# Another order in the slots of the last transformer: rotary sums on GpSimd, roots on ScalarE, the down product one slot later

## The chip, the core and the metric

The kernel runs on one core of one Trainium2 chip. The metric is the device time of one execution in microseconds (us), and runs are compared by their median. TensorE (PE in the profile; PEld are its weight loads), VectorE (DVE), ScalarE (ACT), GpSimd (POOL) and SyncE (SP, which issues DMAs) each carry out their own list of instructions in order. They wait for one another with semaphores, on which an instruction counts up when it has ended.

## The reference

Four layers follow one another on x of 4 x 512 tokens and 128 features. Each computes `x = x + attention(xn) * silu(ffn(xn))`, where xn is the layer norm of x. The change touches only the "ffn" of layer 3, counted from 0, which is itself a transformer of two layers with 8 heads of 64, windows of 64 tokens and a gated feed-forward product. Cut to what matters:

```python
def _layer(x, wqkv, qs, ksc, wo, lg, lb, w1, b1, w2, b2):
    h = shift_token(x)                    # half of the features come from the token before
    q, k, v = jnp.split(h @ wqkv, 3, axis=-1)
    q, k, v = (to_heads(q), to_heads(k), to_heads(v))
    q = l2norm(q) * qs                    # t / max(norm(t), 1e-12)
    k = l2norm(k) * ksc
    q, k = rotary_xpos(q, k)              # q * cos * scale + rotate_half(q) * sin * scale; k with 1 / scale
    o = local_attention(q, k, v)          # softmax over the own window and the one before
    x = x + o @ wo
    h = shift_token(x)
    h = (h - mu) / jnp.sqrt(var + 1e-05) * lg + lb
    a, g = jnp.split(h @ w1 + b1, 2, axis=-1)
    x = x + (a * gelu(g)) @ w2 + b2
    return x
```

## The kernel before

All data are float32. `transformer` is called once, by `ffn3`, with depth 2, 8 heads, window 64 and a hidden width of 341 (three chunks, `HC`). The 2048 tokens are 16 tiles of 128. With 8 heads a tile is one group (`NG == 1`), so the two layers make 32 groups, numbered n, G or t alike.

`slots()` yields one slot after another, and in each slot several groups stand at several stages: `ahead` (slot s works on group s + 2: projections, squares, norms, rotation), `turn` (group s + 1: rotated queries and keys are transposed), `now` (group s: scores, softmax, weighting with the values, transposed outputs), `tail` (group s - 1: product with `w_o`, first residual sum, layer norm), `ffn` (group s - 2: gate and up product, gelu, down product) and `last` (group s - 3: the second residual sum). Every engine has its own loop over the slots, and what stands in such a loop, in that order, is the engine's list; nothing else sets the order.

What the steps of the prediction name, with lines of before:

- Rotation: `sums` (L680, L682) on VectorE adds up squares and floors them; GpSimd raises them to the power -0.5 (L404, twice in a slot, for queries and keys); `normalise` (L689) on VectorE multiplies the projection by that; GpSimd multiplies by cosines (L415) and by sines (L416, L417, halves); VectorE adds the two products in the next slot (L715); TensorE transposes the sum (`turn_qk`, L492), and ScalarE copies it to `qT` or `kT` (L651, L654, L655).
- Attention: `score` (L468 for the mask, L475), VectorE maximum and difference (L704, L706), ScalarE exponential (L606), `turn_p` (L484), copies to `pT` (L616), `weigh` (L502), VectorE reciprocal and product (L735, L737), `turn_o` (L510), copy to `oT` (L661).
- Head mixing: `mix_heads` (L524), first residual sum on VectorE (L723), transpose (L579), layer norm statistics (L740, L742, L744), GpSimd's root (L407), `ln` (L751), transpose (L556), ScalarE copy (L613).
- Feed-forward: `gate_up` (L534), gelu on ScalarE (L645), product on VectorE (L729), `down` (L544), second residual sum (L698).
- ScalarE's tables: a load (L641) before the gelus and one (L657) behind them, each brought on by a one-element operation on `spare`.
- Banks: `T` has two halves, which `T_job` hands out in turn to the transposes and to the gate and up products; whoever takes a half waits until what stood in it was read. `misc` is one bank for `yT`, `sh2`, `lnP` and `fT`. For that reason `down(t)` waits for `lnd.at(t + 1, 4)`, the end of L751 of the next group.

`transformer32`, the transformer of layer 2, is another function and stays as it is. It has forms of instructions that the change brings here: a sum of the rotary products on GpSimd (L1024 there), the root by a logarithm and an exponential on ScalarE (L1235, L1237), and normalising by a product of three factors on VectorE (L1359).

## Time and profile before

| | us |
|---|---|
| median of 3 runs | 3855.44 (3849.27 to 3860.63) |
| the profiled execution, its own time | 3847.89 |
| its span in the profile | 3846.1 |
| first to last score of the changed function | 3402.17 to 3791.43 = 389.26 |
| last instruction of its last residual sum ends | about 3823.3 |

Times in the profile are counted from the start of the span. An interval "idle before" is an engine's idle time ahead of an instruction, and the name behind an arrow is what ended it. The start of a slot is read here at the first mask product of `score` (L468), so that the differences of these starts are the lengths of the slots.

### The profile page before, as it was taken

The numbers are of one execution on the slowest core, as the hardware profiler recorded it, in microseconds if no ns is written. First come the engines' busy times: TensorE is split into PE (matmuls) and PEld (weight loads), VectorE is DVE, ScalarE is ACT, GpSimd is POOL, SyncE is SP. The second block draws the span as 40 slices with busy tenths as digits, with TensorE's granted clock in tenths as the row PEclk, the third lists the DMA queues.
The fourth block names the chain that finished last, engine by engine and source line by source line (L and its number), as shares of the span: only waits on it lengthen the run. The fifth ranks groups of instructions, "written<-read, shape, count | busy, mean of one in ns | idle before, by whom it ended". The sixth has DMA issues, their size and how long they took to land. (4 is left out here: it accounts for less than half of the span.)

```text
span 3846.1 us, 125062 instructions
## 1 busy us (share of the span) xinstructions
PE 3488.5 (91%) x52643; PEld 2407.4 (63%) x52653; DVE 2484.3 (65%) x5535; ACT 2288.7 (60%) x4664; POOL 1778.5 (46%) x1846
## 2 busy tenths in 40 slices
PE   7996999999799997999999999999999996968885
PEld 4664555544466664676677677677677774846664
DVE  4446455510566655777777777777777774568885
ACT  2323655522455555777677777777777775457775
POOL 2003000000121126677676776776776773177773
PEclk9997999999799998999999999999999997989998
DMA  1000000010000002211221211221211211121100
GB/s 27 2 3 25 1 1 1 1 31 4 5 2 2 2 2 66 75 47 49 73 49 47 76 49 47 75 49 47 76 49 48 50 47 23 31 81 24 23 22 21
DMA packets 156331, 130.10 MB, mean 34 GB/s; under 512 B 53592, under 2 KB 146304, under 8 KB 154880
## 3 DMA queue, kind: packets, MB, share of 16 engines
q1 hardware_dynamic: 155776, 122.09, 12.3%
q8 instruction: 423, 6.93, 0.8%
q14 instruction: 132, 1.08, 0.1%
HBM read 31.93 MB, written 3.54 MB: 9 GB/s over the span
## 5 line engine op out<-in xcount | busy, mean ns | idle before, releaser
L1072 PE MATMUL t_wa<-t_w_qkv,t_resid 128*128 128x512 f32 x1152 | 584.5, 608 | 21.7 <-DMA t_scales<-in_L_ffn_k_scale 19.0
L1334 DVE TENSOR_REDUCE t_ssq<-t_sq 128x8 f32<-128x512 f32 x384 | 260.9, 679 | 134.4 <-ACT t_sq L1223 134.4
L1027 POOL TENSOR_TENSOR t_ra<-t_ra,t_rb 128x512 f32<-128x512 f32 x192 | 244.0, 1271 | 194.5 <-DVE t_rb L1352 194.5
L1223 ACT ACTIVATE t_sq<-t_wa 128x512 f32<-128x512 f32 x384 | 226.6, 590 | 151.3 <-PE t_wa L1072 151.3
L3109 DVE TENSOR_REDUCE a_nmax<-a_A 128x2 f32<-128x1024 f32 (+3 forms) x256 | 206.1, 823 | 127.0 <-PE a_A L3007 124.7
L1110 PEld LDWEIGHTS t_T<-ident,t_ra 128*128 128x128 f32 x1536 | 177.2, 141 | 145.0 <-issue 135.3
L1389 DVE TENSOR_REDUCE t_nmax<-t_S 128x8 f32<-128x512 f32 x192 | 132.8, 691 | 196.9 <-PE t_S L1094 189.2
L1072 PEld LDWEIGHTS t_wa<-t_w_qkv,t_resid 128*128 128x128 f32 x1152 | 188.3, 197 | 109.8 <-issue 94.4
L1110 PE MATMUL t_T<-ident,t_ra 128*128 128x128 f32 x1536 | 239.3, 279 | 14.5 <-ACT t_qT L1250 10.2
L1024 POOL TENSOR_TENSOR t_ra<-t_ra,t_rb 128x512 f32<-128x512 f32 x192 | 244.4, 1273 | 15.1
L3102 POOL TENSOR_SCALAR_AFFINE_SELECT a_pt<-a_pt 128x512 f32<-128x512 f32 x128 | 79.7, 634 | 370.1 <-ACT a_pt L3082 370.1
L3082 ACT ACTIVATE a_pt<-a_B 128x512 f32<-128x512 f32 (+1 forms) x384 | 176.5, 528 | 118.5 <-PE a_B L3018 118.4
L1030 POOL TENSOR_TENSOR t_ra<-t_ra,t_inv 128x512 f32<-128x512 f32 x192 | 200.1, 1042 | 97.6 <-ACT t_inv L1237 89.9
L1013 POOL TENSOR_TENSOR t_ra<-t_kn,t_rot 128x512 f32<-128x512 f32 x192 | 244.3, 1273 | 0.0
L1121 PEld LDWEIGHTS t_S<-t_vw,t_pT 64*32 64x32 f32 x9216 | 134.5, 106 | 129.4 <-issue 129.2
L2527 POOL COPY a_rep<-a_rden 128x512 f32<-128x512 f32 x32 | 19.6, 614 | 389.5 <-DVE a_rden L2556 389.5
L1140 PE MATMUL t_misc<-t_oT,t_w_o 128*128 128x128 f32 x1536 | 198.7, 283 | 0.9 <-DVE t_resid L1383 0.9
L1121 PE MATMUL t_S<-t_vw,t_pT 64*32 64x66 f32 x9216 | 164.2, 226 | 37.3 <-ACT t_pT L1247 33.8
L1140 PEld LDWEIGHTS t_misc<-t_oT,t_w_o 128*128 128x128 f32 x1536 | 180.4, 193 | 10.1 <-issue 1.2
L2536 DVE TENSOR_REDUCE a_nmax<-a_A 128x2 f32<-128x1024 f32 (+3 forms) x128 | 102.3, 820 | 125.9 <-PE a_A L2406 125.9
L2475 ACT ACTIVATE a_p<-a_A,a_nmax 128x512 f32<-128x512 f32 (+3 forms) x256 | 133.3, 534 | 84.0 <-DVE a_nmax L2536 84.0
L3018 PE MATMUL a_B<-a_Q,a_K 32*128 32x384 f32 (+3 forms) x1024 | 182.3, 451 | 1.0 <-ACT a_pt L3082 0.6
(506 smaller groups left out, 9747.6 us busy)
## 6 DMA issues: line engine op xcount, KB each, us to landing
t_vw<-t_vn SPq DMA_DIRECT2D x768, 66.0 KB, 2.0
t_vw<-t_vn SPq DMA_DIRECT2D x672, 33.0 KB, 2.3
t_w_qkv<-in_L_ffn_Wqkv SPq DMA_DIRECT2D x6, 1536.0 KB, 6.6
t_v<-t_vn SPq DMA_DIRECT2D x56, 132.0 KB, 2.9
t_vw<-t_nothing SPq DMA_DIRECT2D x96, 33.0 KB, 2.3
t_w_o<-in_L_ffn_Wo SPq DMA_DIRECT2D x6, 512.0 KB
f_h<-t_L_ffn_h_w SPq DMA_DIRECT2D x2, 1024.0 KB, 7.4
t_w<-in_L_ffn_W SPq DMA_DIRECT2D x6, 341.0 KB
```

The source lines that it names most:

```text
L1013: pool.tensor_tensor(ra[:, n % 2, 1], kn[:, :], spread(cos, 1, 8), ALU.mult).then_inc(k_rot.sem, 1)
L1024: pool.tensor_tensor(ra[:, mid % 2, 1], ra[:, mid % 2, 1], rb[:, mid % 2, 1], ALU.add).then_inc(k_roped.sem, 1)
L1027: pool.tensor_tensor(ra[:, ahead % 2, 0], ra[:, ahead % 2, 0], rb[:, ahead % 2, 0], ALU.add).then_inc(q_added.sem, 1)
L1030: pool.tensor_tensor(ra[:, ahead % 2, 0], ra[:, ahead % 2, 0], spread(inv[:, ahead % 2, 0:8], 2, HD), ALU.mult).then_inc(q_roped.sem, 1)
L1072: pe.matmul(bank, resid[:, b, lo:lo + P], w_qkv[:, l % 2, at:at + 512], start=True, stop=True).then_inc(wa_up.sem, 1)
L1110: m = pe.transpose(bank[:, j * P:(j + 1) * P], ra[:, n % 2, r, 2 * j:2 * j + 2, :].rearrange("p h d -> p (h d)"), ident[:, :])
L1121: m = pe.matmul(S[W * c:W * c + W, r, j * VD:(j + 1) * VD], pT[rows, j, W * c:W * c + W], values, start=True, stop=True, skip_group_check= ...
L1140: m = pe.matmul(yT, w_o[:, l % 2, c, :], oT[:, c // 4, c % 4, :], start=(c == 0), stop=(c == 4 * NG - 1))
L1223: act.activation(sq[:, r].rearrange("p h d -> p (h d)"), wa[:, WA[kind], :], ACT.Square).then_inc(squared.sem, 1)
L1334: v.tensor_reduce(ssq[:, n % 2, 8 * r:8 * r + 8, 0], sq[:, r], X, ALU.add).then_inc(summed.sem, 1)
L3018: m = pe.matmul(bank[:, at:at + (TPB - kt) * P], K[rows, u % HELD, 16 * kt:16 * kt + 16, :].rearrange("p t r -> p (t r)"), Q[rows, u % HEL ...
L3109: v.tensor_reduce(nmax[:, u % 2, t, :].rearrange("p (j e) -> p j e", e=32)[:, 2 * pair:2 * pair + 2, 0], A[:, 2 * pair:2 * pair + 2, 0:(t ...
```

## The change

It touches `transformer` alone, with six parts.

1. The sums of the rotary products go from VectorE (L715) to GpSimd, right behind each group's products.
2. The powers on GpSimd (L404, two of 128x8) go to ScalarE, as one `Ln` and one `Exp` of 128x16 for queries and keys together (`roots`). Both parts of `normalise` wait for this one event, and the factor `LIFT ** 0.5` makes them products of three factors.
3. `down` and its residual sum stand one slot later: TensorE has `down(last)` in the place between `turn_p(now, 1)` and the key transposes, VectorE has L698's operation between the two `sums`. `down` now waits for `lnT_in` of the next group, and `mix_heads(t)` also for `tile_done` of group t - 2.
4. TensorE turns the queries before `turn_p(now, 0)` and the keys before `mix_heads`, where both stood around and behind `weigh`. The feed-forward products stand behind `weigh` and before `turn_o`, where they stood behind `mix_heads`. `T_job` follows this order.
5. On ScalarE the copies of `qT`, `vn` and `kT` and the roots stand before the gelus. The table loads are written out, without the operations on `spare`. There are still two in a slot.
6. On VectorE the product with the gelus (L729) stands last in the slot, and both calls of `normalise` stand ahead of `ln`.

The diff, cut to its core:

```diff
-        for kind, n in (("p0", now), ("p1", now), ("gate", ffn), ("up", ffn), ("q", turn), ("k", turn), ("o", now)):
+        for kind, n in (("q", turn), ("p0", now), ("p1", now), ("k", turn), ("gate", ffn), ("up", ffn), ("o", now)):
...
                 for now, turn, ahead, tail, ffn, last in slots():
-                    if ahead is not None:
-                        n = ahead
-                        for r in range(2):
-                            pool.wait_ge(floored.sem, floored.at(n, r + 1))
-                            pool.tensor_tensor(inv[:, n % 2, r, :], ssq[:, n % 2, r, :], g["half"][:, 0:8], ALU.pow).then_inc(inved.sem, 1)
                     if tail is not None:
                         pool.wait_ge(lnd.sem, lnd.at(tail, 3))
...
                             pool.tensor_tensor(rb[:, n % 2, r, :, 32:64], qn[:, r, :, 0:32], spread(sin[:, 32:64], 1, 8), ALU.mult).then_inc(sind.sem, 1)
+                            pool.wait_ge(cosd.sem, cosd.at(n, r + 1))
+                            pool.wait_ge(sind.sem, sind.at(n, 2 * r + 2))
+                            pool.tensor_tensor(ra[:, n % 2, r], ra[:, n % 2, r], rb[:, n % 2, r], ALU.add).then_inc(roped.sem, 1)
...
-                    if NG == 1 and t >= 1:
+                    if t >= 1:
                         pe.wait_ge(lnT_in.sem, lnT_in.at(t - 1))
-                    if NG > 1 and t:
-                        pe.wait_ge(tile_done.sem, tile_done.at(t - 1, 2))
+                    if t >= 2:
+                        pe.wait_ge(tile_done.sem, tile_done.at(t - 2, 2))
...
-                    if NG == 1 and t + 1 < NT:
-                        pe.wait_ge(lnd.sem, lnd.at(t + 1, 4))
+                    if t + 1 < NT:
+                        pe.wait_ge(lnT_in.sem, lnT_in.at(t + 1))
...
                     if now is not None:
                         turn_p(now, 1)
+                    if last is not None:
+                        down(last)
+                    if turn is not None:
+                        turn_qk("k", turn)
                     if tail is not None:
                         mix_heads(tail)
...
+                def roots(n):
+                    act.wait_ge(floored.sem, floored.at(n, 2))
+                    act.activation(logs[:, n % 2], ssq[:, n % 2], ACT.Ln, scale=LIFT).then_inc(logged.sem, 1)
+                    act.wait_ge(logged.sem, logged.at(n))
+                    act.activation(inv[:, n % 2], logs[:, n % 2], ACT.Exp, scale=-0.5).then_inc(inved.sem, 1)
...
+                    if ahead is not None:
+                        roots(ahead)
                     if ffn is not None:
-
-                        act.activation(spare[:, 0:1], g["half"][0:1, 0:1], ACT.Gelu)
+                        act.preload_act_table_set("gelu_and_others")
...
-                    v.wait_ge(inved.sem, inved.at(n, r + 1))
+                    v.wait_ge(inved.sem, inved.at(n))
                     if n:
                         v.wait_ge(sind.sem, sind.at(n - 1, 2 * r + 2))
-                    v.tensor_tensor(qn[:, r], wa[:, wa_job[kind, n] % 3, :].rearrange("p (h d) -> p h d", h=8),
-                                    spread(inv[:, n % 2, r, :], 2, HD), ALU.mult).then_inc(normed.sem, 1)
+                    v.scalar_tensor_tensor(out=qn[:, r], in0=spread(inv[:, n % 2, r, :], 2, HD), scalar=LIFT ** 0.5,
+                                           in1=wa[:, wa_job[kind, n] % 3, :].rearrange("p (h d) -> p h d", h=8),
+                                           op0=ALU.mult, op1=ALU.mult).then_inc(normed.sem, 1)
...
-                    if turn is not None:
-                        for r in range(2):
-                            v.wait_ge(cosd.sem, cosd.at(turn, r + 1))
-                            v.wait_ge(sind.sem, sind.at(turn, 2 * r + 2))
-                            v.tensor_tensor(ra[:, turn % 2, r], ra[:, turn % 2, r], rb[:, turn % 2, r], ALU.add).then_inc(roped.sem, 1)
+                    if last is not None:
+                        l, (b, lo) = layer_of(last), columns(last)
+                        v.wait_ge(f_up.sem, f_up.at(last))
```

TensorE, from the scores of one slot on, in the second layer. `t_S` holds scores, `t_wa` the projections, `t_misc<-ident,t_ln` is the transposed `ln`, `t_T<-ident,t_p` the transposed weights of attention. Before:

```order
L468 MATMUL t_S<-t_mask,identb 64x512 x4
L475 MATMUL t_S<-t_kT,t_qT 64x128 x16
L455 MATMUL t_wa<-t_w_qkv,t_resid 128x512
L556 MATMUL t_misc<-ident,t_ln 128x128
L455 MATMUL t_wa<-t_w_qkv,t_resid 128x512
L484 MATMUL t_T<-ident,t_p 128x128 x4
L455 MATMUL t_wa<-t_w_qkv,t_resid 128x512
L484 MATMUL t_T<-ident,t_p 128x128 x4
L524 MATMUL t_misc<-t_oT,t_w_o 128x128 x4
L534 MATMUL t_T<-t_lnT,t_w 128x128 x2
L534 MATMUL t_T<-t_lnT,t_w 85x128
```

TensorE at the same place after the change, as far as head mixing (`t_oT,t_w_o`):

```order
L469 MATMUL t_S<-t_mask,identb 64x512 x4
L476 MATMUL t_S<-t_kT,t_qT 64x128 x16
L456 MATMUL t_wa<-t_w_qkv,t_resid 128x512
L555 MATMUL t_misc<-ident,t_ln 128x128
L456 MATMUL t_wa<-t_w_qkv,t_resid 128x512
L493 MATMUL t_T<-ident,t_ra 128x128 x4
L485 MATMUL t_T<-ident,t_p 128x128 x4
L456 MATMUL t_wa<-t_w_qkv,t_resid 128x512
L485 MATMUL t_T<-ident,t_p 128x128 x4
L545 MATMUL t_misc<-t_hT,t_w 128x128 x3
L493 MATMUL t_T<-ident,t_ra 128x128 x4
L525 MATMUL t_misc<-t_oT,t_w_o 128x128 x4
```

Head mixing now has both transposes of rotated vectors (`ident,t_ra`) and the down product (`t_hT,t_w`) ahead of it; the gate and up products are gone from behind it.

GpSimd, one slot of 32, with `t_inv` the roots for the norms and `t_rstd` the root for the layer norm. Before:

```order
L404 TENSOR_TENSOR t_inv<-t_ssq,half 128x8 x2
L407 TENSOR_TENSOR t_rstd<-t_vare,half 128x1
L415 TENSOR_TENSOR t_ra<-t_qn,t_rot 128x512
L416 TENSOR_TENSOR t_rb<-t_qn,t_rot 128x8x32
L417 TENSOR_TENSOR t_rb<-t_qn,t_rot 128x8x32
L415 TENSOR_TENSOR t_ra<-t_qn,t_rot 128x512
L416 TENSOR_TENSOR t_rb<-t_qn,t_rot 128x8x32
L417 TENSOR_TENSOR t_rb<-t_qn,t_rot 128x8x32
```

GpSimd after the change, the same slot from the layer norm's root on:

```order
L404 TENSOR_TENSOR t_rstd<-t_vare,half 128x1
L413 TENSOR_TENSOR t_ra<-t_qn,t_rot 128x512
L414 TENSOR_TENSOR t_rb<-t_qn,t_rot 128x8x32
L415 TENSOR_TENSOR t_rb<-t_qn,t_rot 128x8x32
L418 TENSOR_TENSOR t_ra<-t_ra,t_rb 128x512
L413 TENSOR_TENSOR t_ra<-t_qn,t_rot 128x512
L414 TENSOR_TENSOR t_rb<-t_qn,t_rot 128x8x32
L415 TENSOR_TENSOR t_rb<-t_qn,t_rot 128x8x32
L418 TENSOR_TENSOR t_ra<-t_ra,t_rb 128x512
```

The two roots for the norms are gone, and each rotation ends with its own sum, so that the sum of the queries stands ahead of all work on the keys.

VectorE, from the first residual sum (`t_resid` of `t_misc`) to the normalising products (`t_qn`). Before:

```order
L723 TENSOR_TENSOR t_resid<-t_misc,t_resid 64x128 x2
L729 SCALAR_TENSOR_TENSOR t_hT<-t_T,t_b,t_gg 128x128 x2
L729 SCALAR_TENSOR_TENSOR t_hT<-t_T,t_b,t_gg 85x128
L735 RECIPROCAL t_rden<-t_S 128x4
L737 TENSOR_TENSOR t_o<-t_S,t_rden 128x4x64
L735 RECIPROCAL t_rden<-t_S 128x4
L737 TENSOR_TENSOR t_o<-t_S,t_rden 128x4x64
L740 BN_STATS t_stats<-t_misc 128x6
L742 BN_AGGR t_mv<-t_stats 128x2
L744 TENSOR_SCALAR t_vare<-t_mv 128x1
L689 TENSOR_TENSOR t_qn<-t_wa,t_inv 128x512
L751 TENSOR_SCALAR t_ln<-t_misc,t_mv,t_rstd 128x128
```

VectorE after the change, the same stretch:

```order
L720 TENSOR_TENSOR t_resid<-t_misc,t_resid 64x128 x2
L725 RECIPROCAL t_rden<-t_S 128x4
L727 TENSOR_TENSOR t_o<-t_S,t_rden 128x4x64
L725 RECIPROCAL t_rden<-t_S 128x4
L727 TENSOR_TENSOR t_o<-t_S,t_rden 128x4x64
L730 BN_STATS t_stats<-t_misc 128x6
L732 BN_AGGR t_mv<-t_stats 128x2
L734 TENSOR_SCALAR t_vare<-t_mv 128x1
L690 SCALAR_TENSOR_TENSOR t_qn<-t_inv,t_wa 128x512 x2
L740 TENSOR_SCALAR t_ln<-t_misc,t_mv,t_rstd 128x128
L746 SCALAR_TENSOR_TENSOR t_hT<-t_T,t_b,t_gg 128x128 x2
L746 SCALAR_TENSOR_TENSOR t_hT<-t_T,t_b,t_gg 85x128
```

The product with the gelus (`t_hT`) moved from ahead of the outputs (`t_o`) to the slot's end, and both normalising products stand together behind the statistics.

## Rows read from the trace of the kernel before

**Rows 1.** Windows: us, busy (instructions) of PE, PEld, DVE, ACT, POOL, clock, DMA.
```profile
3434.70:3588.11 153.41, 134.85 (x1465) 98.38 (x1464) 130.29 (x330) 113.63 (x226) 113.15 (x109) 1.00 0.10 23
```

**Rows 2.** Timeline, TensorE: start, us; where four slots' scores begin.
```profile
3402.17 0.64 PE L468 MATMUL t_S<-t_mask,identb 64*64 64x512 bf16 x4 [0.96 <-ACT t_kT L655]
...
3434.70 0.41 PE L468 MATMUL t_S<-t_mask,identb 64*64 64x512 bf16 x4
...
3588.11 0.41 PE L468 MATMUL t_S<-t_mask,identb 64*64 64x512 bf16 x4
...
3791.43 0.41 PE L468 MATMUL t_S<-t_mask,identb 64*64 64x512 bf16 x4
```

**Rows 3.** Waits, slots in steady state: total us, times, longest.
```profile
PE t_misc L544 <- DVE t_ln L751: 30.1, 27, 1.1
...
DVE t_resid L698 <- PE t_misc L544: 13.3, 27, 0.5
```

**Rows 4.** Timeline, all engines, one slot and the turn into it.
```profile
3519.86 0.17 DVE L735 RECIPROCAL t_rden<-t_S 128x4 f32<-128x4 f32 x1
...
3521.57 0.69 DVE L689 TENSOR_TENSOR t_qn<-t_wa,t_inv 128x512 f32<-128x512 f32 x1
...
3522.34 1.27 POOL L415 TENSOR_TENSOR t_ra<-t_qn,t_rot 128x512 f32<-128x512 f32 x1
...
3522.87 0.91 PE L544 MATMUL t_misc<-t_hT,t_w 128*128 128x128 f32 x6 [1.11 <-DVE t_ln L751]
...
3523.70 0.41 PE L468 MATMUL t_S<-t_mask,identb 64*64 64x512 bf16 x4
...
3528.52 0.65 PE L484 MATMUL t_T<-ident,t_p 128*128 128x128 f32 x4
...
3529.01 1.06 PE L524 MATMUL t_misc<-t_oT,t_w_o 128*128 128x128 f32 x8
...
3529.91 1.49 PE L534 MATMUL t_T<-t_lnT,t_w 128*128 128x128 f32 x12
...
3530.79 0.60 DVE L723 TENSOR_TENSOR t_resid<-t_misc,t_resid 64x128 f32<-64x128 f32 x2
...
3531.35 0.84 ACT L645 ACTIVATE t_gg<-t_T,t_b 128x128 f32<-128x128 f32 x3
...
3532.41 0.66 PE L492 MATMUL t_T<-ident,t_ra 128*128 128x128 f32 x4
```

**Rows 5.** Groups by line: count, busy us, mean ns, idle before.
```profile
L404 POOL TENSOR_TENSOR t_inv<-t_ssq,half 128x8 f32<-128x8 f32 x62 | 112.6, 1821 | 39.0 <-DVE t_ssq L682 38.6
...
L715 DVE TENSOR_TENSOR t_ra<-t_ra,t_rb 128x512 f32<-128x512 f32 x64 | 42.6, 705 | 2.1 <-POOL t_rb L417 2.1
```

**Rows 6.** Timeline, GpSimd in the other transformer, where it adds itself.
```profile
1574.01 1.27 POOL L1013 TENSOR_TENSOR t_ra<-t_kn,t_rot 128x512 f32<-128x512 f32 x1
...
1576.73 1.27 POOL L1024 TENSOR_TENSOR t_ra<-t_ra,t_rb 128x512 f32<-128x512 f32 x1
1577.96 1.27 POOL L1027 TENSOR_TENSOR t_ra<-t_ra,t_rb 128x512 f32<-128x512 f32 x1
```

**Rows 7.** Groups by line, ScalarE in the other transformer.
```profile
L1235 ACT ACTIVATE t_logs<-t_floor_ssq 128x16 f32<-128x16 f32 x22 | 4.7, 216 | 24.2 <-DVE t_floor_ssq L1338 24.1
```

**Rows 8.** Timeline, VectorE and GpSimd where they meet.
```profile
3396.32 1.66 DVE L715 TENSOR_TENSOR t_ra<-t_ra,t_rb 128x512 f32<-128x512 f32 x1 [0.77 <-POOL t_rb L417]
...
3397.39 1.18 POOL L416 TENSOR_TENSOR t_rb<-t_qn,t_rot 128x256 f32<-128x256 f32 x1
...
3416.46 0.74 POOL L417 TENSOR_TENSOR t_rb<-t_qn,t_rot 128x256 f32<-128x256 f32 x1
...
3416.75 0.48 DVE L682 TENSOR_SCALAR t_ssq<-t_ssq 128x8 f32<-128x8 f32 x1
```

**Rows 9.** Timeline, before the first scores.
```profile
3392.04 0.60 ACT L620 ACTIVATE t_vn<-t_wa 128x512 f32<-128x512 f32 x1 [1.11 <-PE t_wa L455]
...
3393.58 1.27 POOL L415 TENSOR_TENSOR t_ra<-t_qn,t_rot 128x512 f32<-128x512 f32 x1
```

More of the change, by code:

```diff
@@ L408, in _ @@
                     if ahead is not None:
+                        n = ahead
                         t = tile_of(n)
@@ L564, in _ @@
                         turn_p(now, 1)
+                    if last is not None:
+                        down(last)
+                    if turn is not None:
+                        turn_qk("k", turn)
                     if tail is not None:
                         mix_heads(tail)
[L567 to L570 removed]
                     if now is not None:
@@ L573, in _ @@
                         weigh(now, 1)
-                    if turn is not None and ffn is not None:
-                        turn_qk("q", turn)
                     if tail is not None:
@@ L579, in _ @@
                         pe.transpose(sh2, resid1[:, b, lo:lo + P], ident[:, :]).then_inc(sh2_up.sem, 1)
-                    if turn is not None:
-                        turn_qk("k", turn)
+                    if ffn is not None:
+                        gate_up(ffn)
                     if now is not None:
                         turn_o(now)
-                    if ffn is not None:
-                        down(ffn)
             @block.scalar
@@ L624, in _ @@
                         exponentials(now, 0)
-                    if ffn is not None and NG == 1:
+                    if ffn is not None:
                         norm_turned(ffn)
@@ L630, in _ @@
                         exponentials(now, 1)
-                    if ffn is not None and NG > 1:
-                        norm_turned(ffn)
+                    if turn is not None:
+                        act.activation(qT[:, turn % 2].rearrange("p j k -> p (j k)"), turned("q", turn), ACT.Copy).then_inc(T_in.sem, 1)
                     if now is not None:
@@ L638, in _ @@
                         copy_p(now, 1)
+                    if ahead is not None:
+                        copy_v(ahead)
+                    if turn is not None:
+                        t, gi = divmod(turn, NG)
+                        src = turned("k", turn).rearrange("p (j k) -> p j k", j=4)
+                        if not first(t + 1):
+                            act.activation(kT[:, (t + 1) % 2, gi, :, 0:window], src[:, :, P - window:P], ACT.Copy)
+                        act.activation(kT[:, t % 2, gi, :, window:window + P], src, ACT.Copy).then_inc(T_in.sem, 1)
+                    if ahead is not None:
+                        roots(ahead)
                     if ffn is not None:
-                        act.activation(spare[:, 0:1], g["half"][0:1, 0:1], ACT.Gelu)
+                        act.preload_act_table_set("gelu_and_others")
                         l = layer_of(ffn)
@@ L751, in _ @@
                         v.tensor_scalar(ln[:, tail % 2, :], sh2, mv[:, 0:1], rstd[:, 0:1], ALU.subtract, ALU.mult).then_inc(lnd.sem, 1)
-                    if ahead is not None and NG == 1:
-                        normalise("k", ahead)
+                    if ffn is not None:
+                        l, j = layer_of(ffn), T_job["up", ffn]
+                        v.wait_ge(T_up.sem, T_up.at(j))
+                        for c, (at, size) in enumerate(HC):
+                            v.wait_ge(gelu_in.sem, gelu_in.at(ffn, c + 1))
+                            v.scalar_tensor_tensor(out=hT[0:size, c, :], in0=T[0:size, j % 2, c * P:(c + 1) * P], scalar=b_1[0:size, l % 2, 0, c:c + 1],
+                                                   in1=gg[0:size, c, :], op0=ALU.add, op1=ALU.mult).then_inc(h_in.sem, 1)
         plained = st.sem("plained")
```

50 lines of the change are left out of this document (12 added, 38 removed).

## The prediction

> **What bounds the kernel now.** The change touches one stage, so I first looked for its slots. Scores begin at 3402.17 in the first of 32 slots and at 3791.43 in the last [rows 2]: 389.26 us for 31 intervals. The last 16 take (3791.43 - 3588.11) / 16 = 12.71 each. In such slots no engine is full: VectorE is busy 130.29 of 153.41 us (85%), TensorE 88%, ScalarE and GpSimd 74% each, at a granted clock of 1.00, which is the 2.4 GHz level [rows 1]. So the bound is a loop of waits. The waits name it: TensorE waits 1.1 us in each slot ahead of the down product for VectorE's `ln`, and VectorE then waits 0.5 us for the down product [rows 3]. The timeline shows the order: down product from 3522.87 to 3523.78, scores right behind it, and VectorE's work, which is nearly dense, leads to the next `ln` [rows 4]. That loop goes through VectorE and TensorE; GpSimd's long roots stand beside it.
>
> **What leaves VectorE and GpSimd.** VectorE loses two rotary sums of about 0.69 us in a slot (705 ns mean) [rows 5], 1.4 us. If VectorE's load were the bound, this would be the gain. GpSimd loses two powers, 3.65 us (1821 ns each) [rows 5], and gains two sums of 1.27 us each, which is what the other transformer's sum takes there [rows 6]: 2.5 us. So its load falls by 1.1 us. The wait of `down` for `ln` also leaves the loop, since `down` stands in the middle of the next slot: 1.1 us of TensorE waiting [rows 3].
>
> **What is late next.** The new order makes a chain that runs once around each slot. The sum of the keys ends on GpSimd, then TensorE turns the keys, mixes heads, VectorE adds the residual, finishes the outputs and statistics, normalises, and only then may GpSimd start the next group. In the kernel before, the turned keys stood behind head mixing and not ahead of it, and the sums were on VectorE. Its length by rows:
>
> - GpSimd, from the start of the queries' cosines: cosines, two half sines and the sum take 1577.96 - 1574.01 = 3.95 us to the next start in the other transformer, its wait for its own products included [rows 6]. Twice is 7.90, and the last ends 0.04 after the next could start: 7.94.
> - Hand-over to TensorE: 0.06. GpSimd itself starts 0.08 after VectorE's normalised queries (3521.57 + 0.69 to 3522.34) [rows 4], so 0.05 to 0.08 is the scale of these.
> - Four transposes of the keys: 0.49, from 3528.52 to 3529.01 [rows 4].
> - Head mixing 1.06, hand-over 0.05, first residual sum 0.60 [rows 4].
> - From the first reciprocal to the normalising of queries, 3519.86 to 3521.57: 1.71, and on to GpSimd's start, 0.77 [rows 4]. The order of these on VectorE is unchanged, and only the product with the gelus, which stood ahead of them, is gone from there.
>
> Together 7.94 + 0.06 + 0.49 + 1.06 + 0.05 + 0.60 + 1.71 + 0.77 = **12.68 us**, as good as the 12.71 of today. So the change trades one loop for another of the same length. An error of 0.03 us in each of the chain's four hand-overs makes 0.12 us; I take 12.55 to 12.85 as bounds.
>
> **Other edits, which the chain hides.** The roots on ScalarE take two operations of about 0.22 us [rows 7] after the keys' floor and are done before VectorE is through with the outputs; uncovered they would cost 0.5 us. They join queries and keys, so the queries' normalising waits for the keys' floor. That floor now stands behind `down` and the second residual sum, and still ends before the first residual sum starts. Normalising by three factors I cost at nothing: it reads the same 128x512. The table loads stay two in a slot; two one-element operations go. The copy of `qT` now stands ahead of `pT` on ScalarE, some 0.5 us on the path from the second exponential to `down`, which ends ahead of the keys. All this lies within what TensorE and VectorE wait for GpSimd.
>
> **Contention.** Where VectorE adds two tensors while GpSimd multiplies, both stretch: the sum took 1.66 us and the half sine behind it 1.18 instead of 0.73. The small floor of the sums (usually 0.17) took 0.48 from 3416.75 and ended at 3417.23, as GpSimd's operation did at 3417.20, and GpSimd lost nothing [rows 8]. After the change VectorE has no such sum, but its floor of the queries falls amid GpSimd's chain in each slot. It may end 0.6 us late, ahead of a wait for `down`; I cost it at nothing, and at 0.45 (1.18 - 0.73) in the rival below. The Trainium skill, GPSIMD Engine Reference, section "Key points", has it that GpSimd shares its SBUF interfaces with VectorE and collides with its two-port modes and with two SBUF inputs. By that every meeting could count, which is rival 3; the trace shows both, one meeting that cost GpSimd 0.45 and one that cost it nothing.
>
> The same page, in "Engine selection", speaks against the change: elementwise additions belong on VectorE, and GpSimd is about twice as slow for two inputs. The trace agrees with the price, 1.27 against 0.69 us, and by it alone each slot would be 1.2 us longer, 35 us in 30 slots. The chain above holds the sums at this price; what pays for it is the wait of `down` that leaves the loop.
>
> **The ends of the stage.** Before the first score: the queries' norm waits today for one power and starts where `vn` is copied (3392.04), with GpSimd's start at 3393.58 [rows 9]. The roots will stand behind that copy (0.60 + 0.43 + hand-overs), so VectorE normalises at about 3393.15 and GpSimd starts at 3393.9; from there 7.94 leads to the keys' transposes at 3401.9, where today they start at 3400.1. That is 1.8 later (0.4 if the copy overlaps). Between first and last score: GpSimd starts its next group about 1.1 after the first score, behind the copies of `kT` and the roots; the first slot has no head mixing (11.1 us in the chain), 30 more have 12.68, and scores start some 0.15 after GpSimd does. 1.1 + 11.1 + 30 x 12.68 + 0.15 = 392.75 against 389.26: 3.5 more. Nearly all comes from the first two slots, which take 9.7 today without feed-forward work and about 12 then, as GpSimd sets them too; VectorE's tables at the second layer (0.8 in today's longest slot) give some back, for VectorE waits anyway. At the end: `down` of the tile before no longer stands ahead of mixing, and 0.9 us [rows 4] is saved, with -3 to 0 as bounds.
>
> Sum: 1.8 + 3.5 - 0.9 = **+4.4 us**. On the profiled execution's own 3847.89 that is 3852.3, and on the median of 3855.44 (0.2% above the profiled one) it is **3859.8**.
>
> **Rivals.**
> 1. GpSimd's chain runs shorter than by rows, or isn't closed. Next in line is TensorE's own loop: scores to the second `turn_p` 4.82, transposes 0.49, `down` 0.91, second residual sum and hand-overs 0.82, mixing, weighing and one transpose to `gate_up` 2.1 (the gap from 3531.4 to 3532.41 is the weighing), half of `gate_up`, gelus and hand-overs 1.8, `turn_o` 0.49 [rows 4], and 0.5 for the copy of `qT`: 11.9. Then 30 x 0.78 is saved: 3859.8 - 23 = 3836. For it: GpSimd's load is only 8.5 of 12.7 us. Against it: every link of the chain is a wait in the code.
> 2. VectorE's load decides, and its 1.4 us are all gained, 30 x 1.4 = 42: 3818. Against it: it needs GpSimd's chain to be hidden.
> 3. Slower: VectorE's floor, now amid GpSimd's rotation, stretches one GpSimd operation in each slot by 0.45 as in [rows 8]. GpSimd's chain decides from the first slot, so all of it counts: 30 x 0.45 = 13.5, to 3873. For it: floor and rotation will meet in each slot, and met rarely before. Against it: in the one meeting shown GpSimd's next operation was not longer.
> 4. The change doesn't do what it says: the logarithm brings a third table load. The order of instructions shows two loads in a slot, and ScalarE would have over 3 us of slack for it: 3860.
>
> **Chances.** The forecast with its bounds 0.62, rival 1 0.13, rival 2 0.05, rival 3 0.15, rival 4 0.05. A measurement tells 0.3% (11.6 us) from no change. Steady slots of 12.55 to 12.85 give -4 to +5, the start and end -4 to +1, and medians scatter by about 5: 3847 to 3870 for the forecast alone. With rival 3 above and part of rival 1 below, 3843 to 3873. Faster by over 0.3%: rival 2, most of rival 1, a little of the forecast, 0.17. Slower: most of rival 3 and a little more, 0.19. Within: 0.64.
>
> **What would show it.** Right: steady slots of 12.6 to 12.8; GpSimd in two runs of four operations, 7.9 us, with a wait of 4 us for VectorE's variance; TensorE waiting 0.5 to 1 us for GpSimd ahead of each turning; VectorE's largest waits for head mixing and for `down`; first two slots of 12 us; no longer any wait of `down` for `ln`. Wrong: slots under 12.4 with TensorE waiting for ScalarE or VectorE instead of GpSimd, or GpSimd operations over their 1.27 and 0.73.

## The result and the profile after the change

The changed kernel takes 3858.3 us (median of 22 runs, 3849.56 to 3870.22) against 3851.78 us before (22 runs): ratio 1.002, 95% interval 1.001 to 1.0029. In a second set it took 3861.92 us (10 runs) against 3850.88 (33 runs): 1.0027, 1.0012 to 1.0041. So it is 6.5 to 11 us slower, within the 0.3% that I had called no change, where +4.4 us was forecast. The profiled execution has a span of 3868.5 us (its own time 3870.22) and was the slowest of the 22. The ratios leave out three executions of the experiments' kernels that took over 7000 us.

In a steady stretch of after no engine is full either. Windows: length, busy (instructions) of PE, PEld, DVE, ACT, POOL, clock, DMA share, GB/s:

```profile
3449.55:3564.00 114.45, 99.44 (x1094) 73.59 (x1094) 89.03 (x224) 85.05 (x168) 74.07 (x80) 1.00 0.09 21
```

VectorE is down from 85% busy [rows 1] to 78%, GpSimd from 74% to 65%. The slot is not shorter for that. The waits of steady slots (us in total, times, longest) show another loop than [rows 3]:

```profile
POOL t_rstd L404 <- DVE t_vare L734: 111.7, 26, 7.3
...
PE t_T L493 <- POOL t_ra L418: 35.8, 52, 1.6
DVE t_resid L711 <- PE t_misc L545: 28.9, 24, 1.3
DVE t_resid L720 <- PE t_misc L525: 23.0, 26, 1.6
```

`down` no longer waits for `ln`. TensorE waits twice a slot for GpSimd's sums, VectorE for `down` and for head mixing, and GpSimd 4.2 us a slot for VectorE's variance. TensorE's wait is 0.36 us ahead of the queries (3543.24) and 0.96 ahead of the keys, where 0.5 to 1 was said for each. One slot on the timeline (start, us, engine, line), which answers [rows 4]:

```profile
3538.36 1.28 DVE L690 SCALAR_TENSOR_TENSOR t_qn<-t_inv,t_wa 128x512 f32<-128x512 f32 x2
3538.51 0.55 POOL L404 TENSOR_TENSOR t_rstd<-t_vare,half 128x1 f32<-128x1 f32 x1 [4.16 <-DVE t_vare L734]
...
3539.13 1.28 POOL L413 TENSOR_TENSOR t_ra<-t_qn,t_rot 128x512 f32<-128x512 f32 x1
...
3539.57 0.41 PE L469 MATMUL t_S<-t_mask,identb 64*64 64x512 bf16 x4
...
3541.05 0.73 POOL L415 TENSOR_TENSOR t_rb<-t_qn,t_rot 128x256 f32<-128x256 f32 x1
...
3541.92 1.27 POOL L418 TENSOR_TENSOR t_ra<-t_ra,t_rb 128x512 f32<-128x512 f32 x1
...
3543.15 1.28 POOL L413 TENSOR_TENSOR t_ra<-t_qn,t_rot 128x512 f32<-128x512 f32 x1
...
3544.39 0.73 POOL L414 TENSOR_TENSOR t_rb<-t_qn,t_rot 128x256 f32<-128x256 f32 x1
3544.57 0.57 DVE L683 TENSOR_SCALAR t_ssq<-t_ssq 128x8 f32<-128x8 f32 x1
...
3545.94 1.26 POOL L418 TENSOR_TENSOR t_ra<-t_ra,t_rb 128x512 f32<-128x512 f32 x1
...
3547.26 0.66 PE L493 MATMUL t_T<-ident,t_ra 128*128 128x128 f32 x4 [0.96 <-POOL t_ra L418]
3547.75 1.06 PE L525 MATMUL t_misc<-t_oT,t_w_o 128*128 128x128 f32 x8
...
3548.85 0.61 DVE L720 TENSOR_TENSOR t_resid<-t_misc,t_resid 64x128 f32<-64x128 f32 x2 [0.85 <-PE t_misc L525]
...
3549.49 0.18 DVE L725 RECIPROCAL t_rden<-t_S 128x4 f32<-128x4 f32 x1
```

This is the chain of the prediction, link by link. GpSimd runs from 3539.13 to 3547.20 (8.07), 0.06 later TensorE turns the keys, mixing stands 0.49 behind, and the residual sum 1.10 behind that. Then come 0.64 to the reciprocal and 1.73 to the next `qn` (L690, read from 3536.63 to 3538.36), and 0.77 from there to GpSimd. The sum is 12.86 us, which is the slot.

The stage by its pieces, each from a timeline. The prologue is from the first projection to the first score, the tail from the last score to the last residual sum. "All three" is the last experiment.

| us | before | before again | after | after again | all three |
|---|---|---|---|---|---|
| prologue | 15.63 | 15.56 | 17.62 | 16.10 | 15.39 |
| first to last score | 389.26 | 392.47 | 403.13 | 401.17 | 385.41 |
| of it a steady slot | 12.71 | 12.71 | 12.86 | 12.86 | 12.42 |
| of it the slot of the second layer's tables, and the next | 26.24 | 27.85 | 29.66 | 27.66 | 24.89 |
| tail | 31.88 | 33.06 | 31.50 | 28.52 | 31.38 |
| sum | 436.8 | 441.1 | 452.3 | 445.8 | 432.2 |

The first traces are 15.5 us apart in this stage, over twice what the medians say. Second traces of the same two kernels are 4.7 apart. The means differ by 10.1, which fits 6.5 to 11. In the code ahead of the stage, which is the same in all of them, executions drift too: its first projection came at 3386.5, 3385.7, 3393.4 and 3391.4 us.

### The profile page after: what moved, and what is told of

Its sections match the earlier page's. It is cut to its first block and busy times, and to the rows that moved or that the text cites. A ratio compares the mean times of both kernels' runs of the same rounds, so it can differ in the third digit from the quotient of the medians.

```text
span 3868.5 us, 124968 instructions
## 1 busy us (share of the span) xinstructions
PE 3497.3 (90%) x52643; PEld 2412.8 (62%) x52653; DVE 2463.0 (64%) x5471; ACT 2293.9 (59%) x4664; POOL 1746.4 (45%) x1846
```

## The experiments

**The keys' sum, half of it.** GpSimd adds only four of the keys' eight heads; the other four are left without their sine products.

```diff
-    pool.tensor_tensor(ra[:, n % 2, r], ra[:, n % 2, r], rb[:, n % 2, r], ALU.add).then_inc(roped.sem, 1)
+    hs = 8 if r == 0 else 4
+    pool.tensor_tensor(ra[:, n % 2, r, 0:hs], ra[:, n % 2, r, 0:hs], rb[:, n % 2, r, 0:hs], ALU.add).then_inc(roped.sem, 1)
```

> The changed kernel with GpSimd's sum of the rotated keys made for four of the eight heads alone (the other four stay unsummed, so part of the keys is wrong). That sum should take about 0.73 us instead of 1.27. Theory A, the loop closes through GpSimd, the key transposes, head mixing, VectorE and back to GpSimd: every steady slot falls from 12.86 by the same 0.54 to 12.32, unless TensorE's own loop (about 12) comes first, 15 us in all. Rival B, VectorE's or TensorE's own work sets the slot: it stays at 12.86.

Measured: 3840.84 us, ratio 0.9981 (0.9968 to 0.9993), steady slot 12.39. The keys' sum takes 0.72 us in place of 1.26, and 0.47 of these 0.54 come out of every slot: GpSimd's chain sets it. The other 0.07 stand in head mixing, which takes 1.13 us here and 1.06 in after; why is not shown.

**The tables of the second layer, in pieces.** VectorE makes one of the six pieces behind `sums("k")` in each of six slots of the first layer, not all six in one slot.

```diff
-    if ahead % SLOTS == 0:
-        make_tables(layer_of(tile_of(ahead)))
+    if ahead == 0:
+        make_tables(0)
...
+    if ahead % SLOTS >= 10 and layer_of(tile_of(ahead)) + 1 < depth:
+        make_tables(layer_of(tile_of(ahead)) + 1, range(ahead % SLOTS - 10, ahead % SLOTS - 9))
```

> The changed kernel with the second layer's rotary tables made earlier: one of the six products in each of six slots, behind the sums of the keys, when GpSimd is through with its rotations. Theory A, the 17.29 us slot at the second layer comes from VectorE's table products meeting GpSimd's rotations, the late residual, and TensorE's clock after its wait: that slot falls to about 12.9, the others stay, 4 us less in all. Rival B, the slot is long for the second layer's weights or its first projection: it stays at 17.

Measured: 3852.93 us, ratio 1.0005 (0.9993 to 1.0017), the slot 12.84 in place of 17.29 (14.75 in the second trace of after, below), the steady slots 12.85. The long slot belongs to the tables, and the pieces cost nothing where GpSimd is idle.

**The keys' sum on VectorE again**, between `sums("q")` and the residual sum of `last`. GpSimd makes the sum for the queries alone. VectorE's part of the edit:

```diff
+    if turn is not None:
+        v.wait_ge(cosd.sem, cosd.at(turn, 2))
+        v.wait_ge(sind.sem, sind.at(turn, 4))
+        v.tensor_tensor(ra[:, turn % 2, 1], ra[:, turn % 2, 1], rb[:, turn % 2, 1], ALU.add).then_inc(kroped.sem, 1)
```

> The changed kernel with the sum of the keys back on VectorE, between the squares' sums of the queries and the second residual sum; the sum of the queries stays on GpSimd. Theory A, GpSimd's chain: it loses 1.27 + 0.14 and the path gains VectorE's 0.70 + 0.05, slots of 12.2 to 12.4, 13 to 18 us less in all. Rival B, VectorE's load decides: slots grow by 0.7 to 13.5, 20 us more. Rival C, GpSimd and VectorE hinder one another in the sum with two inputs from SBUF: it takes up to 1.2 us and the slot stays at 12.8.

Measured: 3845.78 us, ratio 0.9988 (0.9975 to 1.0), steady slot 12.55, less gained than expected. The timeline of this kernel says why:

```profile
3536.98 0.69 DVE L711 TENSOR_TENSOR t_ra<-t_ra,t_rb 128x512 f32<-128x512 f32 x1 [0.77 <-POOL t_rb L416]
3537.59 0.73 DVE L717 SCALAR_TENSOR_TENSOR t_resid<-t_misc,t_b,t_resid 64x128 f32<-64x128 f32 x2
...
3538.46 1.13 PE L527 MATMUL t_misc<-t_oT,t_w_o 128*128 128x128 f32 x8
...
3539.63 0.61 DVE L726 TENSOR_TENSOR t_resid<-t_misc,t_resid 64x128 f32<-64x128 f32 x2 [0.39 <-PE t_misc L527]
```

The sum is shorter by 0.58, but the residual sum now stands behind it, and mixing needs both: it starts 0.73 behind the keys' transposes (3537.73) and not 0.49, and takes 1.13 and not 1.06. With 0.03 less of waiting ahead of the sum this makes 12.86 - 0.58 - 0.03 + 0.24 + 0.07 = 12.56.

**Before, with the sums on GpSimd and nothing else.** The powers, the order and `down` stay as they were; the sums go from VectorE to the place behind each rotation.

> The kernel before with the first part of the change alone: both rotary sums on GpSimd, the powers still there. Theory A, VectorE's load was not what set the slot before, since it waited for the down product and scores: slots stay at 12.7, and the first ones grow to about 11.6, 5 us more in all. Rival B, VectorE's load set the slot: 1.3 us less in each slot, 12 or under, 20 to 40 us less. Rival C, GpSimd with 12.3 us of work in a slot of 12.7 becomes the bound: 13 and more, 10 us more.

Measured: 3855.16 us, ratio 1.0019 (1.0007 to 1.0031), steady slot 12.71, as before to the hundredth. Rival 2 of the prediction stood on VectorE's load, and 1.4 us less of it in each slot are worth nothing there. Nor does GpSimd become the bound (rival C), though it is busy for 103.19 of 113.00 us. All that this part alone costs lies in the first four slots (11.23, 11.25, 15.57, 13.77, before 9.88, 9.55, 13.10, 12.72) and at the tables (15.12, 13.91, before 13.52, 12.71). Part of both stands at a lower clock: 0.61 from 3442 to 3446 us and 0.50 from 3596 to 3600.

**Before and after once more, unchanged.**

> The kernel before once more, unchanged, against itself: a control on how far one profiled execution stands for its kernel. In the first traces the stage of the third layer's transformer (first projection to last residual) took 436.8 us before and 452.3 us after, 15.5 us apart, while the medians of the runs are 6 to 7 us apart. Theory A (the trace of before is representative of its own stage, the earlier stages drift by some us from execution to execution, whatever the kernel): the steady slot 12.71 us, first to last score 389 to 390 us, prologue 15.6, tail 31.9, stage within 1 us of 436.8; the stage's first projection anywhere from 3379 to 3394 us. Theory B (the first trace of before caught a lucky execution of this stage): the stage takes 441 us or more. The ratio of the medians is 1.000 within 0.15% in both.

> The changed kernel once more. Theory A (stage times repeat, only the stages ahead drift): the steady slot 12.86 us, the slot in which the second layer's tables are made 17.3 us, first to last score 403 us, tail 31.5, stage 452 us; ratio 1.001 to 1.003. Theory B (the slot of the tables was a chance event of one execution: its 4.4 us over the steady slot are gone in another): that slot under 14.5 us and the first to last score under 401 us.

Measured: before 3854.48 us against its own 3850.88, ratio 1.0007 (0.9997 to 1.0016); its stage 441.1, just over the border that I had set for a lucky first trace, so theory B held for before. After: stage 445.8, the slot of the tables 14.75 us and not 17.29. Here neither theory held as written: part of the long slot repeats, part is an event of one execution. The first execution of after (start, us):

```profile
3595.01 1.15 DVE L673 TENSOR_TENSOR t_rot<-t_base,t_scales 128x256 f32<-128x256 f32 x1
3595.84 0.91 POOL L414 TENSOR_TENSOR t_rb<-t_qn,t_rot 128x256 f32<-128x256 f32 x1
3596.08 0.81 DVE L674 TENSOR_TENSOR t_rot<-t_base,t_scales 128x128 f32<-128x128 f32 x1
...
3597.62 1.47 POOL L418 TENSOR_TENSOR t_ra<-t_ra,t_rb 128x512 f32<-128x512 f32 x1
3597.88 1.35 DVE L674 TENSOR_TENSOR t_rot<-t_base,t_scales 128x128 f32<-128x128 f32 x1
...
3601.01 2.05 PE L525 MATMUL t_misc<-t_oT,t_w_o 128*128 128x128 f32 x8 [1.22 <-DVE t_resid L711]
```

and the second:

```profile
3594.30 1.35 DVE L674 TENSOR_TENSOR t_rot<-t_base,t_scales 128x128 f32<-128x128 f32 x1
...
3597.44 1.13 PE L525 MATMUL t_misc<-t_oT,t_w_o 128*128 128x128 f32 x8 [1.22 <-DVE t_resid L711]
```

VectorE's table pieces run into GpSimd's rotation in both, with the same durations within 0.01, and mixing waits 1.22 us for the late residual sum in both. In the first execution it starts 1.87 us behind the keys' transposes (3599.14) and not 0.49. These 1.38, and the 0.44 by which GpSimd's rotation of the keys is longer (3594.60 to 3599.09, 4.49 for 4.05), are nearly all of the 1.9 by which the slot of 14.75 is over a steady one. Of after's two executions only the first also has a lower clock behind this wait. Windows of it, the clock behind the five busy times:

```profile
3591.03:3599.00 7.97, 6.37 (x62) 4.00 (x61) 7.75 (x14) 5.61 (x11) 7.68 (x8) 1.00 0.01 2
3599.00:3601.00 2.00, 0.66 (x4) 0.44 (x5) 1.90 (x7) 0.60 (x1) 0.09 (x1) 0.81 0.00 0
3601.00:3604.00 3.00, 2.99 (x26) 2.77 (x28) 1.34 (x4) 1.71 (x3) 0.00 (x0) 0.50 0.00 0
3604.00:3608.00 4.00, 3.84 (x35) 3.52 (x32) 3.43 (x11) 1.24 (x4) 1.46 (x2) 0.62 0.29 68
```

The 0.50 is the level of 1.2 GHz, right after two microseconds in which TensorE was busy for 0.66. Mixing takes 2.05 us in it. In the second execution 3588 to 3603 us has a clock of 1.00. So the meeting makes this slot 1.9 us longer in both executions. The clock adds 2.5 in one, of which the next slot gives back 0.5 (29.66 against 27.66 for the two); the run with the powers had it too (17.31). The clock's part does not belong to the change: the second execution of before has it at the same place, without any meeting, and its two slots take 27.85 us and not 26.24. A window of that execution:

```profile
3587.00:3591.00 4.00, 4.00 (x44) 3.08 (x44) 1.38 (x4) 0.55 (x2) 4.00 (x6) 0.61 0.32 76
```

**Both of the best single changes.** The keys' sum on VectorE, and the tables in pieces.

> After with two things changed: the sum of the keys' rotary products on VectorE again, between the queries' and the keys' sums of squares, as in the run with that alone; and the second layer's tables made one piece in each of six slots, as in the run with that alone. Theory A (the two costs are separate: GpSimd's 1.27 us of the keys' sum on the loop, and the meeting of VectorE's tables with GpSimd's rotation in one slot): steady slot 12.55 us, no long slot at the second layer (12.6 to 13.0), first to last score 388 to 390 us, tail about 29 us, stage 434 to 437 us; time 3 to 6 us under the kernel before in the same chip's runs (ratio 0.9985 to 0.9992). Theory B (the pieces now meet a VectorE that has no free time, since it bounds the loop in this form): the six slots with a piece take 0.5 us more each, and nothing is left over the run with the sum alone (ratio 0.9988).

Measured: 3849.11 us, ratio 0.9992 (0.9983 to 1.0001), steady slot 12.56, no long slot (12.57, 12.62), first to last score 389.29. The slots bear out that the two costs add up, and the pieces do not lengthen their slots. The time is 1.8 us under before and not 3 to 6, with 1 inside the interval. The tail was 31.42, not 29.

**The roots as powers on GpSimd again.** After with its second part undone; `normalise` has two factors again, and waits for its own power.

```diff
+    for r in range(2):
+        pool.wait_ge(floored.sem, floored.at(n, r + 1))
+        pool.tensor_tensor(inv[:, n % 2, r, :], ssq[:, n % 2, r, :], g["half"][:, 0:8], ALU.pow).then_inc(inved.sem, 1)
...
-    if ahead is not None:
-        roots(ahead)
```

> After with its second part undone: the inverse norms of queries and keys are powers on GpSimd again (two of 128x8, 1.64 us each in the trace of before), and ScalarE has no Ln and Exp pair for them. Theory A (GpSimd waits 4.2 us a slot for VectorE's variance, and the two powers, 3.3 us, fit into this wait: the floor of the keys is there 3.2 us before the variance): the steady slot stays at 12.86 us within 0.05; first to last score 403 us within 2. So the roots' move to ScalarE neither gains nor costs here. Theory B (GpSimd's whole load sets the slot): 12.86 + 3.3 = 16.1 us at the most, anything above 13.1 speaks for it. Theory C (the powers slow VectorE's operations on SBUF beside them): 0.2 to 0.5 us a slot more with GpSimd still waiting.

Measured: 3862.16 us, ratio 1.0028 (1.0016 to 1.0039), steady slot 12.86, as in after. GpSimd of this kernel:

```profile
3549.16 3.25 POOL L404 TENSOR_TENSOR t_inv<-t_ssq,half 128x8 f32<-128x8 f32 x2
3553.36 0.55 POOL L407 TENSOR_TENSOR t_rstd<-t_vare,half 128x1 f32<-128x1 f32 x1 [0.95 <-DVE t_vare L728]
```

The powers fill 3.25 us of the wait and leave 0.95 of it. Moving the roots to ScalarE, with the product of three factors that goes with it, neither gains nor costs in this order.

**One semaphore for GpSimd's products**, so that its sum waits once and not twice. VectorE's normalising waits for this semaphore too, once as before.

```diff
-    pool.wait_ge(cosd.sem, cosd.at(n, r + 1))
-    pool.wait_ge(sind.sem, sind.at(n, 2 * r + 2))
+    pool.wait_ge(rotd.sem, rotd.at(n, 3 * r + 3))
```

> After with one change: cosines and half sines on GpSimd raise one semaphore, so that GpSimd's sum waits for one semaphore of its own engine and not for two. In the traces of after this sum starts 0.14 us behind the end of the second half sine; in the other transformer, whose sum waits for one semaphore, it starts 0.09 behind. Theory A (the second wait costs GpSimd about 0.07 us each, and GpSimd's chain sets the slot): each rotation 3.95 us to the next start in place of 4.02, steady slot 12.72 us (12.70 to 12.80), first to last score 4 us less than after at the same slot at the second layer. Theory B (the 0.07 comes from something else, such as the other operands): slot 12.86 as before.

Measured: 3852.82 us, ratio 1.0003 (0.9993 to 1.0014), steady slot 12.72. GpSimd of this kernel:

```profile
3549.77 0.72 POOL L414 TENSOR_TENSOR t_rb<-t_qn,t_rot 128x256 f32<-128x256 f32 x1
3550.57 1.27 POOL L416 TENSOR_TENSOR t_ra<-t_ra,t_rb 128x512 f32<-128x512 f32 x1
```

The sum starts 0.08 behind the half sine, in after 0.14 (3541.05 + 0.73 to 3541.92). Twice these 0.06 is 0.12 of the 0.14 by which the slot is shorter.

**Both sums on VectorE, in the new order.** The keys' sum stands where it stood in the run with that alone; the queries' sum:

```diff
+    if turn is not None:
+        v.wait_ge(cosd.sem, cosd.at(turn, 1))
+        v.wait_ge(sind.sem, sind.at(turn, 2))
+        v.tensor_tensor(ra[:, turn % 2, 0], ra[:, turn % 2, 0], rb[:, turn % 2, 0], ALU.add).then_inc(roped.sem, 1)
```

> After with both rotary sums on VectorE again (the queries' behind the softmax's subtractions, the keys' behind the queries' sum of squares), all else as in after. GpSimd's part of the loop is then 2 x 2.7 = 5.4 us in place of 8.07. Theory A (VectorE's in-order queue becomes the bound: it was nearly dense in the run with the keys' sum alone, 12.55 us a slot, and the queries' sum now stands between the softmax and the queries' transposes, which is on the path to the down product, the residual and the mixing): steady slot 13.0 to 13.6 us, VectorE idle under 1.5 us of it, GpSimd waiting over 6 us; first to last score 405 to 420 us. So the new order alone loses, and the sums' move pays for it. Theory B (without the sums GpSimd leaves the path and TensorE's own loop decides): 11.9 to 12.3 us a slot.

Measured: 3867.53 us, ratio 1.004 (1.0024 to 1.0056), steady slot 13.45, as theory A says, but VectorE is not dense. Its timeline, with one row of GpSimd:

```profile
3539.40 0.68 DVE L703 TENSOR_TENSOR t_ra<-t_ra,t_rb 128x512 f32<-128x512 f32 x1
3539.47 1.20 POOL L416 TENSOR_TENSOR t_rb<-t_qn,t_rot 128x256 f32<-128x256 f32 x1
...
3543.24 0.73 DVE L717 SCALAR_TENSOR_TENSOR t_resid<-t_misc,t_b,t_resid 64x128 f32<-64x128 f32 x2 [1.75 <-PE t_misc L543]
```

VectorE waits 1.75 us for `down`, where theory A had it idle for under 1.5 in all. GpSimd is off the loop: its products for the queries ended at 3537.61, 1.8 us before VectorE gets to their sum. By its rows the loop runs from the softmax's maxima through the queries' sum, their transposes, the softmax's transposes, `down`, mixing, the gelus, the turned outputs and the next scores. So the rest of the change without the sums' move loses 0.7 us a slot, the sums' move alone gives nothing, and together they come out near where the kernel was. In the new order the sums' move gains 0.59 (13.45 to 12.86).

**The keys turned late.** TensorE turns them behind `weigh`, and on ScalarE the roots stand ahead of the copies of `kT`.

```diff
-    if turn is not None:
-        turn_qk("k", turn)
     if tail is not None:
         mix_heads(tail)
     if now is not None:
         weigh(now, 0)
         weigh(now, 1)
+    if turn is not None:
+        turn_qk("k", turn)
```

> After with one part of the order undone: the keys are turned behind the weighing and not ahead of the mixing, and on ScalarE the roots stand ahead of the keys' copies. Theory A (the loop through mixing no longer waits for GpSimd's keys, but the keys' copies stand ahead of the gelus on ScalarE, and so ahead of the turned outputs and the next scores: GpSimd's 8.07 us, hand-over and transposes 0.55, copies and gelu about 1.5, turned outputs 0.5, scores to the softmax and on to the next start, follow one another): steady slot 13.5 to 14.0 us, ScalarE waiting for the keys' transposes. Theory B (the chain is cut and GpSimd's rotation runs beside the rest): 11.9 to 12.4 us, with TensorE's own loop as the bound, and this kernel is then 10 us or more faster than before.

Measured: 3894.28 us, ratio 1.0106 (1.0089 to 1.0123), steady slot 14.20. The size is near theory A, the path is not:

```profile
3533.15 1.27 POOL L418 TENSOR_TENSOR t_ra<-t_ra,t_rb 128x512 f32<-128x512 f32 x1
...
3538.36 0.65 PE L493 MATMUL t_T<-ident,t_ra 128*128 128x128 f32 x4
...
3539.33 0.59 ACT L652 ACTIVATE t_kT<-t_T 128x512 f32<-128x512 f32 x1
...
3539.94 1.28 ACT L654 ACT_TABLE_LOAD   x1
...
3542.25 0.63 PE L511 MATMUL t_T<-ident,t_o 128*128 128x128 f32 x4 [1.34 <-ACT t_gg L658]
```

GpSimd is off the loop: the keys' sum ends at 3534.42, and TensorE turns them at 3538.36, without a wait for GpSimd. The keys' copies come late, and the table load for the gelus, the gelus, the turned outputs and the next scores stand behind them. Turning the keys early costs the loop through GpSimd and saves this one.

**All three.** The keys' sum on VectorE, the tables in pieces, and one semaphore. VectorE's sum of the keys then waits once, too, and not twice.

> After with the three changes that gained apart: the keys' sum on VectorE, the second layer's tables made in pieces, and one semaphore for GpSimd's rotation products. Theory A (the costs are separate and the loop still runs through GpSimd's rotation of the queries, where one double wait is left in the run with the first two): steady slot 12.56 - 0.07 = 12.49 us (12.45 to 12.53), no long slot at the second layer, first to last score about 387.2 us, prologue 15.4 to 17; ratio to the kernel before 0.998 to 0.9992, which beats it if only just. Theory B (VectorE's own queue bounds the loop in this form, and not GpSimd): 12.56 us as without the one semaphore.

Measured: 3843.59 us (12 runs) against 3848.45 (17 runs), ratio 0.9987, 95% interval 0.9978 to 0.9996: the only complete kernel of the ones tried here whose interval lies below 1 as a whole, by 0.13%. With so many tried and so near to 1 this is a hint more than a gain. The steady slot is 12.42, 0.14 below the run without the one semaphore and not 0.07: GpSimd's wait and VectorE's wait for the products are each shorter by about 0.06.

## Why the prediction was right, and where its steps failed

**The loop.** It is the predicted one, wait by wait. Its length was predicted as 12.68 and is 12.86, just outside 12.55 to 12.85. The term that was mis-sized is GpSimd's 7.94, which is 8.07: [rows 6] is code whose sum waits for one semaphore, and the changed code waits for two. I had taken the hand-over "its wait for its own products included" without comparing how many waits each has. The one-semaphore run gives 12.72. The small remainder is 0.02 to 0.04 in the two VectorE links.

**What pays for the sums.** The prediction said that the wait of `down`, leaving the loop, pays for the sums' price on GpSimd. The run with both sums on VectorE speaks against it: without the price the slot is 13.45 and not shorter than 12.71. The rest of the change has a longer loop of its own when VectorE makes the sums; with the sums on GpSimd that loop is gone, and the one of 12.86 sets the slot. What `down` one slot later does by itself was not run, nor were the fifth and the sixth part.

**First to last score**, predicted 392.75 and measured 403.13 and 401.17. By GpSimd's starts in the first execution: 1.10 after the first score (1.1 predicted), a first slot of 11.29 (11.1), 27 slots of 12.86 (12.68, +4.9), the two around the tables 29.66 (25.36, +4.3; in the second execution 27.67, +2.3), and 13.84 from the last start to the last score (12.83, +1.0). In this last term the scores stand 0.44 behind GpSimd's start (3539.13 to 3539.57), where I had put 0.15, and the last slot takes 13.39 and not a steady slot's time. The 11.1 was not clean either: the chain's links without head mixing, its hand-over and the residual sum add up to 10.97.

**The tables.** Here a step had the wrong sign. I let VectorE's tables "give some back", for VectorE waits anyway. It does, but the tables stand ahead of both sums of squares and of the residual sum that mixing needs, and they meet GpSimd's rotation, now in front of the chain. Before, GpSimd was idle at that point:

```profile
3578.57 0.42 DVE L672 TENSOR_TENSOR t_rot<-t_base,t_scales 128x256 f32<-128x256 f32 x1
3578.90 0.28 DVE L673 TENSOR_TENSOR t_rot<-t_base,t_scales 128x128 f32<-128x128 f32 x1
```

against 1.15 and 0.81 to 1.35 in after. All six products and their gaps take 1.48 us there (3578.57 to 3580.05) and 4.35 in after (3595.01 to 3599.36). The Trainium skill, GPSIMD Engine Reference, section "Key points", names this case, two SBUF inputs on VectorE beside GpSimd. By the trace the rule decides there, and I had weighed it only for the small floor.

**The floor (rival 3).** The meeting came in every slot, as it said: VectorE's two floors, 172 ns long in steady slots of before, have a mean of 381 ns there now, the queries' 0.57 us and the keys' 0.17. GpSimd did not pay for it. The timeline above shows who did: the floor starts at 3544.57, when the half sine has run since 3544.39, and ends with it, at 3545.14 and 3545.12. Groups of steady slots, count, busy us, mean ns:

```profile
L418 POOL TENSOR_TENSOR t_ra<-t_ra,t_rb 128x512 f32<-128x512 f32 x53 | 67.3, 1270 | 7.6
L414 POOL TENSOR_TENSOR t_rb<-t_qn,t_rot 128x256 f32<-128x256 f32 x53 | 38.8, 732 | 0.0
```

These are the 1.27 of [rows 6] and, within 0.01, the 0.74 of [rows 8]. VectorE's floor ended up to 0.4 us late, ahead of a wait for `down` that covers it, as costed.

**The ends.** The prologue was to be 1.8 longer and is 2.0 and 0.5 longer in the two executions; the mechanism is as told ([rows 9] against these rows of after):

```profile
3398.89 0.60 ACT L617 ACTIVATE t_vn<-t_wa 128x512 f32<-128x512 f32 x1 [1.11 <-PE t_wa L456]
3399.51 0.22 ACT L621 ACTIVATE t_logs<-t_ssq 128x16 f32<-128x16 f32 x1
...
3400.01 1.28 DVE L690 SCALAR_TENSOR_TENSOR t_qn<-t_inv,t_wa 128x512 f32<-128x512 f32 x2 [1.30 <-ACT t_inv L623]
...
3400.85 1.27 POOL L413 TENSOR_TENSOR t_ra<-t_qn,t_rot 128x512 f32<-128x512 f32 x1 [10.50 <-DVE t_qn L690]
```

From `vn` to GpSimd's start it is 1.96 now, 1.54 in [rows 9]. The tail was to be 0.9 shorter and is 0.4 shorter in the first pair, 4.5 in the second. It scatters, so the two pairs do not settle its size. Four microseconds at the 1.2 GHz level lie in it in both kernels (windows of before and of the second execution of after):

```profile
3807.00:3811.00 4.00, 4.00 (x19) 4.00 (x20) 0.58 (x2) 2.00 (x5) 0.00 (x0) 0.50 0.00 0
```

```profile
3816.00:3820.00 4.00, 4.00 (x41) 3.65 (x42) 1.19 (x4) 0.01 (x1) 0.00 (x0) 0.50 0.02 4
```

**The other rivals.** Rival 2 is refuted by the sums' move alone (12.71). Rival 4 is refuted by the count of table loads in after's steady stretch, 26 of L654 and 26 of L660 in 26 slots, and by the unchanged slot with the powers. Rival 1, TensorE's own loop of 11.9, was never reached: the shortest slot, 12.39, still waits for GpSimd, so its size is open.

**The hit is closer than the working deserves.** The median of 3 runs that I started from, 3855.44, is 3.7 us above the median of 22. The difference, 4.4, is 2.1 below the measured 6.5 and 6.6 below the second set's 11.0. The two errors point in opposite directions. The terms of the sum fared worse than their total: by the means of the two pairs of traces they are +1.3, +11.3 and -2.5, where I had +1.8, +3.5 and -0.9. The term between first and last score was mis-sized most, by the steady slot, the tables and the last slot. That the time still fell near the forecast is in part luck.

## What to carry to other kernels

Where a part of the loop goes to an engine that waits, ask whether it comes back into the same chain: four microseconds of idle GpSimd in each slot did not make its 1.27 us free, since they all lie ahead of the wait and the sums behind it. Ask also what the new order would do without the move: here it alone makes the slot 13.45. Before a duration is copied from a similar piece of code, count its waits as well as its operations. And look at the one slot that is different: work that was free beside an idle engine is not free when the other engine works on SBUF at the same time.

## What the runs showed of the hardware that I had not expected

- An operation that waits for two semaphores starts about 0.06 us later than one that waits for one, on GpSimd (0.14 against 0.08 behind its own half sine) and on VectorE (the keys' sum starts 0.11 behind GpSimd's half sine with two waits, 0.04 with one).
- VectorE's products of two SBUF inputs go from 0.42 to 1.15 us (128x256) and from 0.28 to 0.81 and 1.35 (128x128) beside GpSimd, and GpSimd's operations from 0.73 to 0.91 and from 1.27 to 1.47. In another meeting VectorE's sum kept its 0.68 and GpSimd's half sine took all of it, 1.20 for 0.73.
- In the meetings shown here the one that started second paid. The sum that kept its 0.68 had started 0.07 ahead of the half sine of 1.20; 0.12 us in which it still overlapped the end of the half sine before cost it nothing. The product of 1.35 had started 0.26 behind GpSimd's sum, and ended at 3599.23, 0.14 behind it. So which one is longer is told by the order of the starts, and a floor that starts amid GpSimd's half sine costs GpSimd nothing.
- A wait of 1.22 us of TensorE for the residual sum left the clock at 1.00 in one execution and was followed by 0.50, the 1.2 GHz level, in another of the same kernel. One trace of a kernel can be 6.5 us off another of the same kernel in one stage.
